# Four attention stages of a decoder: score tiles of 32 rows, and one score unit for two tiles of tokens

## The reference

```
xn = layernorm(x)                        # per token
q, k, v = xn @ Wq + bq, kv @ Wk + bk, kv @ Wv + bv
s = q_h @ k_h.T / sqrt(8)                # 64 x 64 for each of 16 heads
w = softmax(s)
x = x + concat_h(w @ v_h) @ Wo + bo
```

## Time and profile before

| what | value |
|---|---|
| median of 3 runs | 2318.76 us |
| profiled execution, first to last instruction | 2356.9 us |
| PE, DVE, ACT, POOL busy | 1774.8, 1337.8, 1099.5, 746.9 us |
| phase a1 (729.0 to 908.2) | 179 us |
| phase x2 (1454.0 to 1618.7) | 165 us |
| phase a3 (1697.1 to 1897.0) | 200 us |
| phase x3 (1897.0 to 2061.1) | 164 us |
| mean granted clock of TensorE | 0.857 of full speed |

### The profile page before, as it was taken

How to read it: one execution, slowest core, us unless ns; L and a number is a source line. 1 busy time by engine, 2 the same in 40 slices (tenths; PEclk the granted TensorE clock), 3 DMA queues, 4 the chain that set the end, 5 groups by cost and what they waited for, 6 DMA issues and landing times. The chain is left out here.

```text
span 2356.9 us, 39525 instructions
## 1 busy us (share of the span) xinstructions
PE 1774.8 (75%) x14484; PEld 1215.4 (52%) x14484; DVE 1337.8 (57%) x3646; ACT 1099.5 (47%) x2273; POOL 746.9 (32%) x718
## 2 busy tenths in 40 slices
PE   3887553999895996767999386887788868743994
PEld 1555432435543664644798253565555535542774
DVE  3897587502123774654343365885369969862223
ACT  4775531223243775733344243774357657610441
POOL 1223201360354331146255002330223232165453
PEclk9888885798896998877999697998979969955997
DMA  4111361125623301102376200000000010011224
GB/s 158 83 83 82 104 235 45 49 75 150 161 70 132 124 2 50 37 30 85 110 238 201 75 1 27 28 20 10 3 1 2 2 37 28 11 49 60 62 81 138
DMA packets 145170, 173.18 MB, mean 73 GB/s; under 512 B 21073, under 2 KB 120593, under 8 KB 144049
## 3 DMA queue, kind: packets, MB, share of 16 engines
q1 hardware_dynamic: 125252, 129.09, 17.7%
q0 software_dynamic: 13248, 28.21, 3.6%
q10 hardware_dynamic: 6480, 13.37, 1.5%
HBM read 126.84 MB, written 79.05 MB: 87 GB/s over the span
## 5 line engine op out<-in xcount | busy, mean ns | idle before, releaser
L1154 PE MATMUL a_AV<-a_vx,a_pT 128*64 128x18 f32 (+1 forms) x3072 | 115.1, 224 | 33.0 <-DVE a_two L824 15.3
L1154 PEld LDWEIGHTS a_AV<-a_vx,a_pT 128*64 128x64 f32 x3072 | 105.9, 146 | 62.2 <-issue 28.6
L1016 ACT ACTIVATE a_e<-a_e 128x512 f32<-128x512 f32 x192 | 110.2, 622 | 58.7 <-DVE a_e L846 58.5
L1141 PE MATMUL a_TP<-ident,a_e 128*128 128x128 f32 x768 | 108.0, 285 | 20.0 <-ACT a_e L1016 19.4
L1021 ACT COPY a_pT<-a_TP 128x512 f32<-128x512 f32 x192 | 103.4, 588 | 39.6 <-PE a_TP L1141 39.4
L846 DVE TENSOR_TENSOR a_e<-a_S,a_mx 128x1024 f32<-128x1024 f32 x96 | 117.3, 1222 | 2.9
L1141 PEld LDWEIGHTS a_TP<-ident,a_e 128*128 128x128 f32 x768 | 89.2, 146 | 57.6 <-ACT a_e L1016 48.3
L1130 PE MATMUL a_S<-a_kbd,a_qT 64*64 64x512 f32 x768 | 113.8, 668 | 0.9 <-issue 0.6
L3620 POOL DMA_INDIRECT f_back<-f_ys,f_row x78 | 74.7, 957 | 97.5 <-DVE f_ys L3709 85.6
L3126 POOL DMA_INDIRECT f_back<-f_ys,f_row x80 | 76.6, 957 | 87.1 <-DVE f_ys L3287 66.9
L3759 ACT ACTIVATE f_h<-f_H,f_wt 128x256 f32<-128x256 f32 x156 | 65.2, 473 | 83.5 <-PE f_H L3835 83.5
(11 more groups left out here) (544 smaller groups left out, 4731.4 us busy)
## 6 DMA issues: line engine op xcount, KB each, us to landing
f_wt<-in_f_ew SPq DMA_DIRECT2D x39, 584.0 KB
f_slots<-in_blank SPq DMA_DIRECT2D x1, 18576.0 KB
f_wt<-in_f_leaf SPq DMA_DIRECT2D x94, 98.0 KB, 2.0
f_xs<-f_slots SPq DMA_DIRECT2D x47, 144.0 KB
memory_x_k<-w_stage ACTq DMA_DIRECT2D x24, 256.0 KB, 3.2
f_slots<-in_blank SPq DMA_DIRECT2D x1, 5760.0 KB
f_xs<-leaf_slots SPq DMA_DIRECT2D x22, 256.0 KB
leaf_out<-f_ys SPq DMA_DIRECT2D x22, 256.0 KB
```

Source lines behind the costliest of these rows:

```text
L1016: act.activation(eh, eh, ACT.Exp).then_inc(weights.sem, 1)
L1141: last = pe.transpose(TP[:, half, P * n:P * n + P], ev[:, 4 * half + n, :], k.ident[:, :])
L1154: last = pe.matmul(AV[64 * c:64 * c + 64, 2 * hp * W1:2 * (hp + 1) * W1], pT[:, hp, 64 * c:64 * c + 64], vx[:, g % 2, t, c, 2 * hp:2 * hp ...
```

## The change

A second function `attention_pairs` is added and used for phases 3, 7, 9 and 10 (a1, x2, a3, x3); phase 0 keeps `attention`. In it the step is a pair p of two tiles (t = 0, 1), 16 pairs in a phase.

- Rows are split in four parts of 32 (NR = 4, four heads each), and kbd has four head slots. A new table mask4 takes mask8's place. POOL fills all four slots; ACT's `spread_keys` and the counter `kbd_pool` are gone.
- S is one unit of four banks for the pair: bank r, half t. `score(p)` issues sixteen products of 32 rows by 64 columns over 256 columns, and waits for the second shift of pair p-1.
- DVE: one bias add (a3), one reduce and one maximum (x3) over both tiles, 2048 elements a partition; a shift for each tile; one reciprocal and one multiply for both tiles, AV holding 2 x 144 columns.
- The order changes. PE: turn(p, 0), score(p+1), weigh(p, 0), group work, turn(p, 1), group work, weigh(p, 1), group work. DVE: highest(p), shift(p, 0), take_values(p-1), `between`, shift(p, 1), `behind`. `between` is the mean's shift (even pairs) or the update (odd pairs; in x3 the update is on even ones), `behind` is take_v (even) or the norm statistics (odd). `turn_x(g+2)` now stands at the end of an even pair, with its wait for the update of group g-1, which DVE does in the odd pair that follows.

```diff
+    NR, HR = 4, NH // 4
+    kbd = ph.sb("kbd", [P, 2, 2 * GT, HR, SL])
+    S = ph.ps("S", [P, NR, 2, HR * SL])
...
+            def highest(p):
+                v.wait_ge(scores.sem, scores.after(p))
+                if bias:
+                    links.link(v, v.tensor_tensor(S[:, :, :, :], S[:, :, :, :], bc(bt[:, :, :], 2, [P, NR, 2, HR * SL]), ALU.add))
+                top = mx[:, p % 2, :, :, :].rearrange("p r u h -> p (r u h)")
+                links.link(v, v.tensor_reduce(top, S[:, :, :, :].rearrange("p r u (h j) -> p (r u h) j", j=SL), AX.X, ALU.max))
+                if restricted:
+                    links.link(v, v.tensor_scalar(top, top, 0.0, None, ALU.max))
...
+            for p in range(NPR):
+                highest(p)
+                shift(p, 0)
+                if p:
+                    take_values(p - 1)
+                between(p)
+                shift(p, 1)
+                behind(p)
...
+            for p in range(NPR):
+                g, later = p // 2, p // 2 + 2 < NG
+                exps(p, 0)
+                take_turned(2 * p)
+                if later and p % 2 == 0:
+                    normalize(g + 2, (0, 1))
+                elif later:
+                    take_x(g + 2)
+                exps(p, 1)
+                if p % 2 == 0 and g and finishing:
+                    take_att(g - 1)
+                if later and p % 2:
+                    take_q(g + 2)
+                take_turned(2 * p + 1)
+                if later and p % 2 == 0:
+                    normalize(g + 2, (2, 3))
+                elif later and not cross:
+                    take_k(g + 2)
...
+            def score(p):
+                g, h = p // 2, p % 2
+                if h == 0:
+                    pe.wait_ge(q_ready.sem, q_ready.after(g))
+                    pe.wait_ge(kbd_ready.sem, kbd_ready.after(g))
+                if p:
+                    pe.wait_ge(shifted.sem, shifted.after(2 * (p - 1) + 1))
+                for t in range(2):
+                    for c in range(2):
+                        b = 4 * h + 2 * t + c
+                        for r in range(NR):
+                            rows = slice(32 * r, 32 * r + 32)
+                            last = pe.matmul(S[64 * c:64 * c + 64, r, t, :], qT[rows, g % 2, SL * b:SL * b + SL],
+                                             kbd[rows, g % 2, b, :, :], start=True, stop=True)
+                last.then_inc(scores.sem, 1)
...
+            for p in range(NPR):
+                g, later = p // 2, p // 2 + 2 < NG
+                turn(p, 0)
+                if p + 1 < NPR:
+                    score(p + 1)
+                weigh(p, 0)
+                if p == 0 and not cross:
+                    make_v(1)
+                elif p % 2 == 0 and g and finishing:
...
+                    turn_att(g - 1)
+                elif p % 2 and later:
+                    make_q(g + 2)
+                turn(p, 1)
+                if p % 2 == 0 and g and finishing:
+                    project(g - 1)
+                elif p % 2 and later and not cross:
+                    make_k(g + 2)
+                weigh(p, 1)
+                if p % 2 == 0 and later:
+                    if g and finishing:
+                        pe.wait_ge(x_updated.sem, x_updated.after(g - 1))
...
+                    turn_x(g + 2)
+                elif p % 2 and later and not cross:
+                    make_v(g + 2)
...
+    t["mask4"] = ((p[:, None] // 8) % 4 == np.arange(4)[None, :]).astype(f) * f(8.0 ** -0.5)
```

More of the change, by code:

```diff
@@ L4035, in decoder @@
             0: lambda: attention(nc, k, d, "a0", "a0_q", "a0_k", "a0_v", "a0_o", width=16, diff=0.8 - 0.6 * 2.718281828459045 ** (-3.6), fill="f1"),
-            3: lambda: attention(nc, k, d, "a1", "a1_q", "a1_k", "a1_v", "a1_o", qb="a1_bq", kb="a1_bk", vb="a1_bv", ob="a1_bo", fill="f3"),
-            7: lambda: attention(nc, k, d, "x2", "x2_q", "x2_k", "x2_v", "x2_o", kv="ctx", qb="x2_bq", kb="x2_bk", vb="x2_bv", ob="x2_bo"),
-            9: lambda: attention(nc, k, d, "a3", "a3_q", "a3_k", "a3_v", "a3_o", qb="a3_bq", kb="a3_bk", vb="a3_bv", ob="a3_bo",
+            3: lambda: attention_pairs(nc, k, d, "a1", "a1_q", "a1_k", "a1_v", "a1_o", qb="a1_bq", kb="a1_bk", vb="a1_bv", ob="a1_bo", fill="f3"),
+            7: lambda: attention_pairs(nc, k, d, "x2", "x2_q", "x2_k", "x2_v", "x2_o", kv="ctx", qb="x2_bq", kb="x2_bk", vb="x2_bv", ob="x2_bo"),
+            9: lambda: attention_pairs(nc, k, d, "a3", "a3_q", "a3_k", "a3_v", "a3_o", qb="a3_bq", kb="a3_bk", vb="a3_bv", ob="a3_bo",
                                  affine=("a3_ga", "a3_be"), bias=True),
-            10: lambda: attention(nc, k, d, "x3", "x3_q", "x3_k", "x3_v", kv="ctx", qb="x3_bq", kb="x3_bk", vb="x3_bv",
+            10: lambda: attention_pairs(nc, k, d, "x3", "x3_q", "x3_k", "x3_v", kv="ctx", qb="x3_bq", kb="x3_bk", vb="x3_bv",
                                   restricted=True),
```

374 lines of the change are left out of this document (added).

## The result

| | median, us | range | runs |
|---|---|---|---|
| before | 2320.02 | 2318.24 to 2330.38 | 4 |
| changed | 2370.94 | 2365.95 to 2373.00 | 4 |

The ratio is 1.0202 (95% interval 1.0173 to 1.0231). The predicted 2292, and the whole range of 2272 to 2316, are missed on the other side. The profiled execution of the changed kernel spans 2368.1 us at a mean granted clock of 0.823 (before: 0.857). The one of before was itself 38 us over its median, and the changed one is not, so I compare the four phases, not the spans.

What follows compares the result with a forecast made beforehand. The prediction took a1 as near PE's limit, a3 as DVE's, x2 and x3 between. Five groups -22.5, rest of windows -12, later first shift +6, clock +1.7 made -27: 2318.8 to 2292 us, range 2272 to 2316.

Steps and rivals of the forecast that it cites:

- a little for the clock, +1.7: All four stages: small allowance for a lower PE clock, taking the sum from -28.7 to -27 us.
- the clock falls: Slower rival, x2, x3, a3: a further sixth of their time at 1.2 GHz, +47 us, 2339; 5 in 100.
- 1.00 at 91% busy, 0.97 at 88%, 0.95 at 83%: Stage windows before: PE's granted clock read against its busy share, used to price the slower clock.
- Gaps on PE stay under 2 us, as now: PE in the four stages: pauses were to remain below 2 us, said under the slower-clock rival.
- clock not below 0.93: Sign to check: PE's granted clock in the four stage windows stays at 0.93 or more.
- The rest of the windows (-12): Parts of the four windows outside the five groups: together 12 us shorter.
- First shift later: Stage starts: first reduce (and add) covers two tiles, so +1.4, +1.1, +2.3, +1.0 us, together +6.
- The rest after the last shift: Drain at each stage's end: stays (8.2 us in a1), plus 0.15 us for the wider multiply.
- a smaller gain: Rival: strips overlap less than fully or each pair loses 0.2 us in hand-overs; 2305 us; 22 in 100.
- mean 0.19: DVE in a1's loop after the odd pair's scores: the mean's step takes 0.19 us of the 8.6 us half.
- the first: Slower rival, scores in all pairs: at most four matmuls at once, 2.04 us a pair, 2342; 9 in 100.
- The larger gain: Rival: scores at 1.02 us a pair and hand-overs hidden, -37 us, 2282 and a little below; 12 in 100.

Runs made afterwards that it cites:

- e0: The changed kernel unaltered, run again on another chip beside the follow-ups: 2402.61 us, 1.0222 of the kernel before.
- e1: The changed kernel plus redundant products, read by nobody, where PE would wait in the four stages: 2340.44 us, 0.9953 of the kernel before.
- e10: The changed kernel with e1's redundant products at half their columns, none after the odd pair in x2: 2361.02 us, 1.0024 of the kernel before.
- e9: The kernel before, two score units and order kept, with half the score columns from tile 2 on: 2341.91 us, 0.9947 of the kernel before.
- e6: e1 plus turn x moved behind the odd pair's first turn and more filler from pair 11 on: 2333.41 us, 0.9916 of the kernel before.
- e4: The changed kernel with turn x and its wait for the update moved behind the odd pair's first turn: 2383.60 us, 1.0147 of the kernel before.
- e5: e1 with fp32 transposes instead of products as filler, same places and columns: 2337.49 us, 0.9930 of the kernel before.
- e8: The kernel before with redundant products only at the start of a1, x2, a3 and x3: 2339.60 us, 0.9951 of the kernel before.

## Why the prediction was wrong

**The step that failed** is "a little for the clock, +1.7", and with it the slower rival "the clock falls", which had 5 in 100 and a price of +47. It is what happened, but neither as it was drawn nor at its price. The +47 of the rival stand on top of the forecast of -27 and give 2339; the measured +47 of the four phases stand against the kernel before, so against the forecast the phases are 74 us long. Giving the clock back by filler alone was worth 2.6 in 100, some 60 us (e0 to e1). The step rested on the scale "1.00 at 91% busy, 0.97 at 88%, 0.95 at 83%", and so had only x2, x3 and a3 suffer, and a1 not. The scale is none: a group of x3 before ran at 1.00 with PE busy 14.5 of 17.8 us, 82 in 100, and one of a1 after, busy for 85, follows one with 0.18 of its time at 1.2 GHz. A share of a window mixes groups that run at full clock with groups that do not, and the answer to more or less PE work is a step (e10). The kernel before had such a group to read: x3's first four take 17.8 us at full clock, the fifth takes 19.56 with the clock at 1.2 GHz from 2015.9 to 2022.7, after waits of PE no longer than those of the groups ahead of it (1.06 at most). "Gaps on PE stay under 2 us, as now" was taken as cover. It is false in a3, where the wait for the update is 3.24 us (a1 and x2 have waits of up to 2.6 and 2.2), and where it holds, in x3 (1.96 at most), it was none: two waits of 0.38 and 0.87 us went before the fall. The check that would have shown the mechanism, "clock not below 0.93", failed in all four stages. The Trainium skill (TensorE: Matmul & The Clock Gate, "A second HAM failure mode: psum-queue depth-cycling") describes a kernel whose PE idles briefly between groups and swings between the two levels; the swings above agree, and I had not weighed it.

**What the low clock costs, it costs through the loop.** Before, scores for the next tile lay ready in the second unit. Now every PE piece on the round trip takes 1.7 to 1.9 times as long at 1.2 GHz (weighing 1.14 to 1.90, scores 1.12 to 2.01, turn 1.04 to 1.97), and DVE waits it out. Two units hide part of it, not all: in x3 of e9 a group with 0.38 of its time at 1.2 GHz takes 17.8 us, as the full-clock groups of x3 did before, one with 0.52 takes 19.9. At the low level PE has hardly a pause (the last three rows of x3 above follow each other without one), at 1968.5 the full clock returns, and the pauses with it (1.19 us before the scores at 1976.2); at 1975.3 it falls again.

**The sum at full clock** was nearly right. Scores 1.12 against 1.15, reduce 2.29, reciprocal 0.36 against 0.34, multiply 0.42, update 0.68: all as put. Periods against the forecast: a1 17.9 (17.4), x2 17.3 (16.9), a3 19.6 (19.7, with e1's filler in it), x3 16.15 (16.4). A group saves 4.0 us over the four stages where 4.5 was the term, five groups 20 and not 22.5. The rest of the windows (-12) was mostly not there: e1's windows sum to 553.2 against 569.1, -15.9, so -20 by five groups and +4 by the ends, where the last groups still lose clock (18.2 for one of a1, 20.3 of a3). e6, with more filler there and turn x moved, has 545.1, -24. "First shift later" was 1.4, 0.4, 2.4, 0.4, with a1 and a3 as forecast. The rest after the last shift was +5.2, not +0.6. So with the clock held in the loops the change is worth 0.5 to 0.8 in 100 (e1, and e6 with e4's move), 11 to 20 us, not 27: on its own the rival "a smaller gain", within the range.

**What made a1 17.9 and not 17.4.** From the scores at 790.18 to those at 799.48 are 9.3 us, forecast 8.6; the other half is 8.6, forecast 8.8 (its terms add up to 8.9). The term is "mean 0.19": the mean's step takes 1.04 in a1 now, and 0.15 before. POOL's four key products start at 796.11 and take 1.04 each, 4.04 together, so the second runs from 797.11 to 798.15; the mean's step starts at 797.13 and ends at 798.17. The order of the pairs moved it there. In x2, where it met POOL in three of five groups, it takes up to 1.21:

```profile
1460.32 1.27 POOL L1350 TENSOR_TENSOR x<-x,rows 128x512 f32<-128x512 f32 x1
1460.40 1.21 DVE L1383 SCALAR_TENSOR_TENSOR x_nmr<-x_mv,x_rstd 128x4 f32<-128x4 f32 x1
1461.64 1.23 DVE L1426 TENSOR_TENSOR x_e<-x_S,x_mx 128x1024 f32<-128x1024 f32 x1
```

It ends with POOL's instruction (at 1461.61 and 1461.59), and the second shift waits behind it. A move past POOL's work was priced by its duration in another place. That a placement without the overlap gives a1 the half microsecond was not tried.

**ACT** was as forecast in kind: the spread is gone and costs nothing; its busy time fell by 13 to 15 us a window and not 23. The 23 are a whole stage's 32 copies; in a1's window before there are only 25 of them, 17.6 us, the first groups' having run ahead of the first shift, and the rest of ACT's work grew a little. **Rivals:** the first is out (1.12 us). The larger gain isn't seen either.

**Open:** what amount or pattern of pauses brings the clock down isn't settled. e9 against the changed kernel shows that the smaller work counts and so does the rest of the change, where the single unit's waits are the likely part, not tested by themselves; x2 at full clock in e9 and half of its time below in the changed kernel, with the same score work, is not taken apart further. The same waits stand in groups with and without a fall, in x3 before as in x3 after, so what decides between them is not in one group's waits.

## What to carry to other kernels

Before work is taken off an engine whose clock is granted by its activity, look at each stage group by group, not at its mean: count the pauses left between its pieces and price every piece on the round trip at the lower level (here 1.7 to 1.9 times) too. If the clock then falls, redundant work in the waits can bring it back: 2.6 in 100 here, with a different amount in each stage, while the same kind of work in the loop itself did not pay. Look first for one long wait that a change of order takes away (a3: 171 to 157 us). A second buffer that hides a dependency loop hides part of a slower clock as well.

## What the runs showed of the hardware

- Eight strips of 32 rows by 64 columns run side by side: sixteen fp32 products over 256 columns, 32 MATMULs and 32 loads, in 1.12 us, 35 ns each, next work 1.05 after the start. An eighth of their 8192 columns is 1024, for which the q product alone takes 0.96.
- As filler in the waits, fp32 transposes hold the clock as well as fp32 products do (windows at 0.93 to 0.98 with either, 0.71 to 0.89 without; e5, e1, e0).
- A DVE instruction of 4 elements a partition that reads two SBUF tensors, started while a POOL tensor product runs, ends with that product: 1.04 and 1.21 us against 0.15 free. It was so wherever the two met in the four stages, before as well (0.79 in x2, 0.95 in a3). The shifts, which read PSUM, take 1.22 beside POOL as without it. The Trainium skill (SBUF — State Buffer, "SBUF: two separate sides") says that DVE, with two SBUF inputs, and GpSimd take a shared pair of ports in turn for a whole instruction; the trace agrees.
- A phase's start is a chain with PE mostly idle, at a granted clock of 0.52 to 0.56 in the kernel before. With filler it is at 0.83 to 0.90, and the kernel takes 0.5 in 100 less (e8).
